# A new order in front of a fused conv and quantised-dense kernel: kernel blocks first, split convs, an early bias row

## The chip, the cores and the metric

One core of a Trainium2 chip. The metric is device microseconds of one execution. The engines are TensorE (PE; PEld is its weight load), VectorE (DVE), ScalarE (ACT), GpSimd (POOL) and the queue engine SyncE (SP). Each works through its own list of instructions in order; they meet only at semaphores.

## What is computed

`x` is 64 samples of 64 channels of 1024. A grouped convolution (9 taps, 4 groups) with a term from `cond` gives rows, these go through a dense layer whose operands are rounded to 8-bit levels, and the rounded result is added to `x`:

```
h  = conv1d(x, weight, groups=4, padding=4) + (cond @ c_weight.T)[:, :, None] + cbias
hq = fake_quant(h, 8 bits, per row)           # round(h / s) * s, s = absmax / 127
kq = fake_quant(kernel, 8 bits, per column)   # kernel is 1024 x 1024
y  = hq @ kq + fake_quant(bias, 16 bits, per row)
out = x + fake_quant(y, 8 bits, per row)
```

## The kernel before

The work is 32 tiles of 128 rows (8 samples x 16 channels of one group). The dense kernel comes as 8 blocks of 128 columns, loaded in four pairs of 1 MB. Step k of each engine's hand-written list handles several tiles at once: conv(k) on TensorE, the levels of tile k, dense of tile k - 2 for its first 512 columns (h = 0), dense of tile k - 4 (k - 3 and k - 2 later on) for its second half (h = 1), and the output of an older tile. `seconds(k)` gives the tiles whose second half falls in step k: one each, but two in steps 13 and 18, so that `outs(k)`, the y that are rounded in step k, has two in steps 15 and 20.

What a tile passes through:
- SP loads `xwin`; ScalarE rounds it to `x_hi` (`round_x`); POOL makes `x_lo = xwin - x_hi` (`split`, L229). SP's next load of a slot waits for that split.
- TensorE's `conv(t)` (L404): two select matmuls, then four matmuls each with x_hi and w_hi, x_hi and w_lo, x_lo and w_hi. The last four wait for `lo_made`.
- VectorE's `column_max(t)` (L602), TensorE's `spread_max(t)` (L429), VectorE's `levels(t)` (L619): the inverse, and the rounding of half of the tile to `a_int`; the other half is ScalarE's `round_levels(t)` (L325), four instructions.
- TensorE's `turn_levels(t)` (L437) transposes the integers into `turn_ps`, ScalarE's `take_levels(t)` (L317) copies them to `a_t`, and `dense(t, h)` (L447) multiplies with `kq` into bank h of `dense_ps`.
- VectorE's `scale_half(t, h)` and `add_bias` (VectorE for h = 0, POOL for h = 1), VectorE's `out_scale`, ScalarE's `quantise(t)` (two instructions, L335), POOL's `add_x(t)`, SP's store.

The kernel blocks come in front, among the first steps. VectorE's `k_levels(pair)` (L555) takes the absolute maximum of a pair, its scale and inverse, and rounds those of its blocks that are in `DVE_K`; ScalarE's `k_round(fb)` rounds the blocks in `ACT_K`. TensorE's `k_turn(user)` (L461) transposes a block into a bank of `dense_ps`, and ScalarE's `k_take(user)` copies it from there to `kq`. There are ten users, in the order of `K_USERS`: eight blocks, and two that spread the scales over the partitions ("scale0", "scale1"). A turn waits for an earlier user's take, so that its bank is free. `b_row`, the bias on all 128 partitions, is loaded late by SP, and `bias_scale` and `bias_levels` work on it in steps 1 and 2.

TensorE's list in front is, before: warm_up, ctx matmuls, warm_up, conv(0), k_turns 0-1, spread(0), conv(1), k_turns 2-4, spread(1), turn_levels(0), conv(2), dense(0,0), turn_levels(1), k_turns 5-6, spread(2), conv(3), k_turns 7-8, dense(1,0), turn_levels(2), spread(3), k_turn 9, conv(4), turn_levels(3), dense(2,0), spread(4), dense(0,1), conv(5). VectorE's: k_levels(0), column_max(0), k_levels(1), levels(0), column_max(1), k_levels(2), levels(1), bias_scale, column_max(2), k_levels(3), scale_half(0,0), levels(2), and so on.

Of the kernel before, what the change touches and what calls it, by code (L numbers as in the profile page):

```python
# [13 lines left out]
P = 128  # L14
# [7 lines left out]
NS = P // CG  # L22
# [10 lines left out]
ACT_K = (1, 3)  # L33
DVE_K = (0, 2, 4, 5, 6, 7)
# [4 lines left out]
def build(nc, xw, xr, wt, cond_t, cw_t, cond_bias, ker, bias, out):  # L39
    with ExitStack() as ctx:  # L40
# [6 lines left out]
        def sem(name):  # L47
# [27 lines left out]
        b_row = sb("b_row", [P, F], F32)  # L75
# [27 lines left out]
        turn_ps = ps("turn_ps", [P, NS, P], I16)  # L103

# [5 lines left out]
            "k_turned", "k_taken", "b_max_made", "b_scale_made", "b_inv_made",  # L110
# [53 lines left out]
        def _(sp):  # L164
# [51 lines left out]
        def _(pool):  # L216
# [50 lines left out]
        def _(act):  # L267
            act.dma_start(condt[:], cond_t).then_inc(s["cond_in"], 16)
# [40 lines left out]
            def bias_levels():  # L309
                act.wait_ge(s["b_inv_made"], 1)  # L310
                act.activation(b_int[:], b_row[:], ACT.Copy, scale=b_stat[:, 2:3]
# [45 lines left out]
            for k in range(second_step(LAST) + 2):  # L357
                if k == 2:
                    take_levels(1)
                    k_take(5)  # L360
                    k_take(6)
                    round_x(4)
                    bias_levels()
                elif k == 3:
                    k_take(7)
                    k_take(8)
                    take_levels(2)
                    round_x(5)
                else:
                    if k == 4:  # L370
                        k_take(9)
                    if there(k - 1):
                        take_levels(k - 1)
                    if there(k + 2):
                        round_x(k + 2)
                if k == 0:
                    k_round(3)
                    k_take(2)
                    k_take(3)
                    k_take(4)  # L380
                for t in outs(k):
                    quantise(t)
                if there(k):
                    round_levels(k)
            quantise_last()

        @block.tensor
        def _(pe):
            def warm_up():
                for i in range(WARM):  # L390
                    pe.matmul(dense_ps[:, 1, :].rearrange("p (i f) -> p i f", f=P), ident[:],
# [4 lines left out]
            warm_up()  # L396
            pe.wait_ge(s["cond_made"], 1)
# [6 lines left out]
            def conv(t):  # L404
                at, g, n0 = t % 2, t % GROUPS, t // GROUPS * NS
                x_at = t % XSPLIT
                wait(pe, "a_rounded_dve", t - 1)
                wait(pe, "a_rounded", t - 1)
                wait(pe, "hi_made", t + 1)
                for hs in range(2):  # L410
                    ns = slice(n0 + hs * NH, n0 + (hs + 1) * NH)
                    mm = pe.matmul(  # L412
                        conv_ps[:, at, hs, :].rearrange("p (n b) -> p n b", n=NH),
                        ctx2[:, g].rearrange("k q o -> k (q o)"),
                        select[:, ns].unsqueeze(2).to_broadcast([P, NH, BLOCKS]),
                        start=True, stop=False, skip_group_check=True)
                for x, w in ((x_hi, w_hi), (x_hi, w_lo), (x_lo, w_hi)):
                    if x is x_lo:
                        wait(pe, "lo_made", t + 1)
                    for ch in range(2):  # L420
# [6 lines left out]
                mm.then_inc(s["conv_made"], 1)  # L427
# [9 lines left out]
            def turn_levels(t):  # L437
                wait(pe, "a_rounded_dve", t + 1)
                wait(pe, "a_rounded", t + 1)
                wait(pe, "a_made", t)  # L440
                for j in range(NS):
# [5 lines left out]
            def dense(t, h):  # L447
# [5 lines left out]
                if t == 0:  # L453
                    pe.wait_ge(s["k_taken"], k_taken_of(f"scale{h}"))
# [6 lines left out]
            def k_turn(user):  # L461
                wait(pe, "k_taken", user if user > 5 else user - 1)
# [21 lines left out]
            pe.wait_ge(s["w_lo_made"], 2)  # L484
# [7 lines left out]
            for k in range(TILES):  # L492
                again = seconds(k)
                if k == 4:
                    k_turn(9)
                conv(k)
                if k == 0:
                    k_turns(0, 1)
                if k == 1:
                    k_turns(2, 4)  # L500
                if k == 3:
                    k_turns(7, 8)
                if k in (2, 3):
                    dense(k - LAG, 0)
                    turn_levels(k - 1)
                    if k == 2:
                        k_turns(5, 6)
                    spread_max(k)
# [240 lines left out]
```

## Time and profile before

| | |
|---|---|
| three runs, median (lowest to highest) | 283.77 us (283.61 to 284.38) |
| profiled execution, its own time | 282.26 us |
| its span, first to last instruction | 280.5 us |
| mean granted TensorE clock | 0.976 of full speed |
| busy: PE, DVE, ACT, POOL | 253.2, 211.9, 185.0, 194.2 us |
| HBM | 38.99 MB read, 16.78 MB written |

The rows below come from the page of this execution and from its trace. A granted clock of 1.00 is 2.4 GHz and 0.50 is 1.2 GHz. The busy time of an engine is the union of its instructions; TensorE's instructions overlap in the pipeline, so the time that one group costs is read from its start to the start of the next. A line in order of time may stand for several like instructions (x4): its second number is then the time from the first's start to the last's end. "[1.63 <-ACT x_hi L291]" is idle time ahead of it and what ended it.

### The profile page before, as it was taken

Reading aid. Unit: us, or ns where it says so; the run is one execution under the profiler, and the core shown is the slowest. Engines: PE = TensorE matmul, PEld = TensorE weight load, DVE = VectorE, ACT = ScalarE, POOL = GpSimd, SP = SyncE. Lnnn points to the kernel's source line nnn. Section 1 sums busy time; section 2 is a strip of 40 time slices with the busy share of each in tenths; the row PEclk is TensorE's granted clock in tenths of the full one; section 3 lists DMA queues with packets and bytes.
Section 4 is the critical chain, followed back from the end, with each engine's and each line's share of the span. In section 5 each row is a group of like instructions: output and inputs, shape, how many; then the busy total and the mean of one; then the engine's idle time right before and its main releaser. Section 6 shows DMA issues by size and latency. Waiting matters only on the chain.

```text
span 280.5 us, 4237 instructions
## 1 busy us (share of the span) xinstructions
PE 253.2 (90%) x1372; PEld 165.0 (59%) x1372; DVE 211.9 (76%) x447; ACT 185.0 (66%) x278; POOL 194.2 (69%) x104
## 2 busy tenths in 40 slices
PE   7966869999999999999899999799999999999800
PEld 3555557666666666666566566566666666665300
DVE  2598974668777778777978677967778888777674
ACT  4257686446777767667986567867777777755662
POOL 3533332544888888879897788997888888845973
PEclk9979999999999999999999999999999999999975
DMA  6999323530566665646677645565666664444424
GB/s 230 407 411 355 103 92 141 167 137 0 196 220 199 222 211 201 195 167 198 226 272 256 188 155 198 211 239 213 227 225 225 221 232 152 150 151 152 151 116 183
DMA packets 15800, 56.05 MB, mean 200 GB/s; under 512 B 1954, under 2 KB 1954, under 8 KB 15778
## 3 DMA queue, kind: packets, MB, share of 16 engines
q1 hardware_dynamic: 15488, 55.71, 56.2%
q8 instruction: 11, 0.18, 0.3%
q10 hardware_dynamic: 290, 0.07, 0.1%
q14 instruction: 11, 0.09, 0.1%
HBM read 38.99 MB, written 16.78 MB: 199 GB/s over the span
## 4 chain that ended last, share of the span: by engine, by line
POOL 49%; issue 41%; DVE 3%; DMA 3%; ACT 1%; SPq 0%; POOLq 0%; DVEq 0%; PE 0%
POOL x_lo L233 26%; POOL y L241 15%; POOL o_sb L249 8%; DMA k_raw<-ffn_kernel 3%; DVE k_max L558 1%; ACT kq L305 1%; DVE o_sb L665 1%; DVE y_max L656 0%; ACT x_hi L291 0%; SPq L175 0%; DVE k_int L569 0%; DVE dense_ps L590 0%; ACT y_int L349 0%; DVE y L599 0%; DVE last_max L673 0%
## 5 line engine op out<-in xcount | busy, mean ns | idle before, releaser
L456 PE MATMUL dense_ps<-kq,a_t 128*128 128x512 bf16 x496 | 116.7, 379 | 0.0
L233 POOL TENSOR_TENSOR x_lo<-xwin,x_hi 128x1032 fp32r<-128x1032 f32 x32 | 76.6, 2393 | 51.6 <-ACT x_hi L291 51.6
L249 POOL TENSOR_TENSOR o_sb<-y,o_sb 128x1024 f32<-128x1024 f32 x31 | 73.9, 2386 | 24.6 <-ACT y L341 24.6
L456 PEld LDWEIGHTS dense_ps<-kq,a_t 128*128 128x128 bf16 x496 | 47.6, 101 | 45.1 <-issue 0.3
L604 DVE TENSOR_REDUCE small_ps<-conv_ps 128x8 f32<-128x1024 f32 x32 | 39.4, 1232 | 39.6 <-PE conv_ps L422 39.5
L321 ACT CAST a_t<-turn_ps 128x1024 bf16<-128x1024 int16 x32 | 32.4, 1012 | 48.7 <-PE turn_ps L442 48.7
L338 ACT ACTIVATE y_int<-y,y_inv 128x1024 int16<-128x1024 f32 x31 | 35.6, 1147 | 24.1 <-DVE y_inv L647 24.1
L241 POOL TENSOR_TENSOR y<-y,bq 128x512 f32<-128x512 f32 x33 | 41.8, 1273 | 1.0 <-DVE y L590 1.0
L656 DVE TENSOR_REDUCE y_max<-y 128x1 f32<-128x1024 f32 x31 | 37.5, 1211 | 2.3 <-POOL y L241 2.0
L330 ACT ACTIVATE a_int<-conv_ps,inv 128x128 int16<-128x128 f32 x128 | 36.1, 363 | 1.9 <-DVE inv L625 1.9
L291 ACT CAST x_hi<-xwin 128x1032 fp32r<-128x1032 f32 x32 | 33.8, 1055 | 5.3 <-DMA xwin<-x_windows 5.3
L341 ACT ACTIVATE y<-y_int,y_scale 128x1024 f32<-128x1024 int16 x31 | 35.7, 1151 | 1.0
L422 PE MATMUL conv_ps<-x_hi,w_hi 128*128 128x512 f32 x128 | 36.3, 406 | 0.0
L422 PE MATMUL conv_ps<-x_hi,w_lo 128*128 128x512 f32 x128 | 35.8, 401 | 0.0
L422 PE MATMUL conv_ps<-x_lo,w_hi 128*128 128x512 f32 x128 | 35.2, 397 | 0.0
L422 PEld LDWEIGHTS conv_ps<-x_hi,w_lo 128*128 128x128 f32 x128 | 24.5, 192 | 6.2
L422 PEld LDWEIGHTS conv_ps<-x_hi,w_hi 128*128 128x128 f32 x128 | 25.0, 196 | 5.0
L422 PEld LDWEIGHTS conv_ps<-x_lo,w_hi 128*128 128x128 f32 x128 | 24.1, 188 | 6.1
L412 PE MATMUL conv_ps<-select,ctx 128*128 128x512 f32 x64 | 26.0, 489 | 1.6 <-ACT x_hi L291 1.6
L590 DVE SCALAR_TENSOR_TENSOR dense_ps<-dense_ps,row_scale,k_scale_b 128x512 f32<-128x512 f32 x31 | 23.1, 744 | 4.9 <-PE dense_ps L456 4.9
L442 PE MATMUL turn_ps<-ident_b,a_int 128*128 128x128 bf16 x256 | 19.8, 220 | 5.2 <-issue 3.5
L590 DVE SCALAR_TENSOR_TENSOR y<-dense_ps,row_scale,k_scale_b 128x512 f32<-128x512 f32 x31 | 23.0, 743 | 1.4 <-PE dense_ps L456 1.4
(62 smaller groups left out, 209.1 us busy)
## 6 DMA issues: line engine op xcount, KB each, us to landing
xwin<-x_windows SPq DMA_DIRECT2D x32, 516.0 KB, 4.7
o_sb<-x_rows SPq DMA_DIRECT2D x32, 512.0 KB, 4.5
out<-o_sb SPq DMA_DIRECT2D x31, 512.0 KB, 2.9
k_raw<-ffn_kernel SPq DMA_DIRECT2D x4, 1024.0 KB, 11.9
w_raw<-taps SPq DMA_DIRECT2D x2, 256.0 KB, 3.0
b_row<-ffn_bias SPq DMA_DIRECT2D x1, 512.0 KB, 15.1
out<-o_sb SPq DMA_DIRECT2D x2, 256.0 KB, 2.7
condt<-cond_t ACTq DMA_DIRECT2D x1, 32.0 KB
```

The lines of the kernel that those rows point to most:

```text
L233: pool.tensor_tensor(x_lo[:, at].rearrange("p n b -> p (n b)"), xwin[:, t % XWIN, :], x_hi[:, at].bitcast(F32).rearrange("p n b -> p (n b) ...
L241: pool.tensor_tensor(y[:, t % YRING, half(h)], y[:, t % YRING, half(h)], bq[:, half(h)], ALU.add).then_inc(s["biased1" if h else "biased0_ ...
L249: pool.tensor_tensor(o_sb[:, at, :], y[:, t % YRING, :], o_sb[:, at, :], ALU.add).then_inc(s["o_made"], 1)
L291: act.copy(x_hi[:, t % XSPLIT].rearrange("p n b -> p (n b)"), xwin[:, t % XWIN, :]).then_inc(s["hi_made"], 1)
L330: ins = act.activation(a_int[:, at, n * BLOCKS:(n + 1) * BLOCKS], conv_cols(at)[:, n, :], ACT.Copy, scale=inv8[:, at, n:n + 1])
L338: act.activation(y_int[:, t % 2], y[:, t % YRING, :], ACT.Copy, scale=y_inv[:, t % 2:t % 2 + 1]).then_inc(s["y_rounded"], 1)
L341: act.activation(y[:, t % YRING, :], y_int[:, t % 2], ACT.Copy, scale=y_scale[:, t % 2:t % 2 + 1]).then_inc(s["y_dequantised"], 1)
L422: mm = pe.matmul(conv_ps[:, at, hs, :].rearrange("p (n b) -> p n b", n=NH), w[:, ch, g].rearrange("p q o -> p (q o)"), x[:, x_at, hs * NH: ...
L456: mm = pe.matmul(dense_bank(t, h), a_t[:, t % LEVELS, q].rearrange("b j o -> b (j o)"), kq[:, q, half(h)], start=(q == 0), stop=(q == Q - 1))
L590: dve.scalar_tensor_tensor(out=to, in0=dense_bank(t, h), scalar=row_scale[:, t % RSRING:t % RSRING + 1], in1=k_scale_b[:, half(h)], op0=AL ...
L604: dve.tensor_reduce(cmax_ps, conv_ps[:, t % 2].rearrange("p h (n b) -> p (h n) b", b=BLOCKS), AX_X, ALU.max, apply_absolute_value=True).th ...
L656: dve.tensor_reduce(y_max[:, at], y[:, t % YRING, :], AX_X, ALU.max, apply_absolute_value=True).then_inc(s["y_max_made"], 1)
```

## The change

- The bias is loaded as one row (4 KB) by ScalarE's queue, first of all. After the first warm-up TensorE spreads it over the partitions with two fp32 matmuls of one row into both banks of `dense_ps`; VectorE and ScalarE read it there. `bias_scale` is VectorE's work ahead of the ctx instructions, `bias_levels` ScalarE's behind round_x(0). SP's loads are now x(2) ahead of k pair 3.
- `ACT_K` is (0, 1, 5, 7), `DVE_K` (2, 3, 4, 6). The scales of a pair are two instructions of one column.
- "scale0" is the third of `K_USERS` and has a bank of its own, `turn_ps`.
- conv is in two parts for tiles 1 to 4: `conv_start` (select and x_hi with w_hi), `conv_rest`.
- Tiles 0 and 1 are rounded by VectorE alone (`WHOLE = 2`).
- POOL's split(1), split(3) and split(4) wait for VectorE's 2nd, 3rd and 4th block rounding.
- The lists of the first five steps are written out anew on TensorE, VectorE and ScalarE.
- On ScalarE, in a step with two y, round_levels stands between the two quantises.

```diff
-ACT_K = (1, 3)
-DVE_K = (0, 2, 4, 5, 6, 7)
+ACT_K = (0, 1, 5, 7)
+DVE_K = (2, 3, 4, 6)
+WHOLE = 2
...
         def k_bank(user):
-            return dense_ps[:, user % 2 if user < 5 else 1, :]
-
-        K_USERS = (0, 1, 2, 3, "scale0", 4, 5, 6, 7, "scale1")
+            if user == 2:
+                return turn_f32
+            return dense_ps[:, 0 if user in (0, 3) else 1, :]
+
+        K_USERS = (0, 1, "scale0", 2, 3, 4, 5, 6, 7, "scale1")
...
             load_k(2)
+            load_xwin(2)
             load_k(3)
-            load_xwin(2)
-            sp.dma_start(b_row[:], bias.partition_broadcast(P)).then_inc(s["b_in"], 16)
             load_xwin(3)
...
             def split(t):
                 wait(pool, "hi_made", t + 1)
+                wait(pool, "k_rounded_dve", {1: 2, 3: 3, 4: 4}.get(t, 0))
                 wait(pool, "conv_made", t - XSPLIT + 1)
...
         def _(act):
+            act.dma_start(b_row[:], bias.unsqueeze(0)).then_inc(s["b_in"], 16)
             act.dma_start(condt[:], cond_t).then_inc(s["cond_in"], 16)
...
             round_x(0)
+            bias_levels()
+            k_round(0)
             k_round(1)
-            k_take(0)
-            k_take(1)
             round_x(1)
...
+            for user in range(5):
+                k_take(user)
+            round_x(2)
+            take_levels(0)
+            round_x(3)
+            take_levels(1)
+            round_x(4)
+            k_round(5)
+            k_take(5)
+            round_levels(2)
+            take_levels(2)
+            k_take(6)
+            round_x(5)
+            k_round(7)
+            round_levels(3)
+            k_take(7)
+            k_take(8)
+            take_levels(3)
+            k_take(9)
+            round_x(6)
+            round_levels(4)
+            for k in range(5, second_step(LAST) + 2):
+                if there(k - 1):
+                    take_levels(k - 1)
+                if there(k + 2):
+                    round_x(k + 2)
+                for t in outs(k)[:1]:
                     quantise(t)
                 if there(k):
                     round_levels(k)
+                for t in outs(k)[1:]:
+                    quantise(t)
...
             warm_up()
+            pe.wait_ge(s["b_in"], 16)
+            for h in range(2):
+                pe.matmul(dense_ps[:, h, :], ones[0:1, :], b_row[:, half(h)], start=True, stop=True
+                          ).then_inc(s["b_spread"], 1)
...
             def k_turn(user):
-                wait(pe, "k_taken", user if user > 5 else user - 1)
+                wait(pe, "k_taken", user if user >= 5 else (0, 0, 0, 1, 2)[user])
+                if user == 0:
+                    pe.wait_ge(s["b_rounded"], 1)
...
+            conv(0)
+            k_turns(0, 2)
+            conv_start(1)
+            k_turns(3, 4)
+            spread_max(0)
+            conv_rest(1)
+            turn_levels(0)
+            conv_start(2)
+            spread_max(1)
+            conv_rest(2)
+            turn_levels(1)
+            dense(0, 0)
+            conv_start(3)
+            spread_max(2)
+            conv_rest(3)
+            k_turn(5)
+            turn_levels(2)
+            dense(1, 0)
+            k_turn(6)
+            conv_start(4)
+            spread_max(3)
+            conv_rest(4)
+            k_turns(7, 8)
+            turn_levels(3)
+            k_turn(9)
+            dense(2, 0)
+            spread_max(4)
+            dense(0, 1)
+            for k in range(5, TILES):
...
-                dve.tensor_scalar(k_scale[:, fs], k_max[:, fs], 1.0 / 127, TINY, ALU.mult,
-                                  ALU.max).then_inc(s["k_scale_made"], 1)
-                dve.wait_ge(s["k_scale_made"], pair + 1)
+                for fb in (2 * pair, 2 * pair + 1):
+                    dve.tensor_scalar(k_scale[:, fb:fb + 1], k_max[:, fb:fb + 1], 1.0 / 127, TINY,
+                                      ALU.mult, ALU.max).then_inc(s["k_scale_made"], 1)
...
             k_levels(0)
-            for k in range(TILES):
+            k_levels(1)
+            column_max(0)
+            levels(0)
+            column_max(1)
+            levels(1)
+            column_max(2)
+            scale_half(0, 0)
+            k_levels(2)
+            levels(2)
+            add_bias(0, 0)
+            column_max(3)
+            scale_half(1, 0)
+            k_levels(3)
+            levels(3)
+            add_bias(1, 0)
+            for k in range(4, TILES):
```

## Rows read from the trace of the kernel before

**Rows 1.** Busy times by stretch: length, engines' busy us (x instructions), granted clock, DMA share, GB/s.
```profile
16.00:17.70 1.70, 0.09 (x1) 0.00 (x0) 1.70 (x1) 1.66 (x2) 0.00 (x0) 1.00 1.02 406
...
17.70:21.10 3.40, 3.38 (x8) 2.72 (x9) 3.30 (x5) 0.25 (x1) 2.38 (x1) 0.50 1.03 414
...
39.45:42.70 3.25, 1.04 (x17) 0.86 (x17) 2.06 (x3) 2.79 (x6) 1.11 (x1) 1.00 0.32 98
...
60.00:67.34 7.34, 7.34 (x42) 4.82 (x41) 5.19 (x12) 3.17 (x7) 3.66 (x3) 1.00 0.00 0
...
130.00:150.00 20.00, 18.59 (x104) 12.14 (x103) 15.59 (x34) 15.00 (x25) 17.91 (x9) 1.00 0.61 216
```

**Rows 2.** In order of time, the front: start, us, engine, line, operation; then idle time and releaser.
```profile
6.19 3.78 PE L391 MATMUL dense_ps<-ident 128*128 128x512 f32 x4
...
6.30 0.22 DVE L542 CAST ctx_r<-small_ps 128x64 fp32r<-128x64 f32 x1 [4.07 <-PE small_ps L400]
...
7.08 0.69 DVE L547 TENSOR_TENSOR ctx<-small_ps,ctx_r 64x512 fp32r<-64x512 f32 x1
...
29.41 1.21 DVE L575 TENSOR_REDUCE b_stat<-b_row 128x1 f32<-128x1024 f32 x1
...
30.84 0.17 DVE L581 RECIPROCAL b_stat<-b_stat 128x1 f32<-128x1 f32 x1
```

**Rows 3.** In order of time: VectorE's kernel levels, a split beside one, and a scale_half.
```profile
17.74 2.38 POOL L233 TENSOR_TENSOR x_lo<-xwin,x_hi 128x1032 fp32r<-128x1032 f32 x1 [6.18 <-ACT x_hi L291]
...
17.82 2.32 DVE L561 TENSOR_SCALAR k_scale<-k_max 128x2 f32<-128x2 f32 x1
...
24.25 2.27 DVE L558 TENSOR_REDUCE k_max<-k_raw 128x2 f32<-128x2048 f32 x1
...
26.96 1.42 DVE L569 TENSOR_SCALAR k_int<-k_raw,k_inv 128x1024 int16<-128x1024 f32 x2
...
36.73 0.75 DVE L590 SCALAR_TENSOR_TENSOR dense_ps<-dense_ps,row_scale,k_scale_b 128x512 f32<-128x512 f32 x1
```

**Rows 4.** In order of time: ScalarE's first two takes.
```profile
14.79 1.93 ACT L305 CAST kq<-dense_ps 128x1024 bf16<-128x1024 int16 x2 [0.32 <-PE dense_ps L478]
```

**Rows 5.** In order of time: TensorE in a steady step, and the second scale turn.
```profile
45.14 1.11 PE L469 MATMUL dense_ps<-ident,k_scale 128*128 128x128 f32 x8
...
60.59 0.78 PE L412 MATMUL conv_ps<-select,ctx 128*128 128x512 f32 x2
...
62.16 1.11 PE L422 MATMUL conv_ps<-x_hi,w_lo 128*128 128x512 f32 x4
...
64.05 0.62 PE L442 MATMUL turn_ps<-ident_b,a_int 128*128 128x128 bf16 x8
...
64.51 1.89 PE L456 MATMUL dense_ps<-kq,a_t 128*128 128x512 bf16 x8
...
66.23 0.33 PE L433 MATMUL small_ps<-col_max,same_b 128*128 128x64 f32 x2
```

**Rows 6.** In order of time: dense(0,0), and the beginning of conv(5).
```profile
31.08 1.90 PE L456 MATMUL dense_ps<-kq,a_t 128*128 128x512 bf16 x8
...
53.26 0.78 PE L412 MATMUL conv_ps<-select,ctx 128*128 128x512 f32 x2
```

**Rows 7.** In order of time: step 15, the second quantise's neighbours and TensorE's turn.
```profile
137.41 0.21 DVE L625 RECIPROCAL inv<-small_ps 128x8 f32<-128x8 f32 x1
...
139.56 1.12 ACT L330 ACTIVATE a_int<-conv_ps,inv 128x128 int16<-128x128 f32 x4
...
140.79 0.61 PE L442 MATMUL turn_ps<-ident_b,a_int 128*128 128x128 bf16 x8 [1.41 <-issue]
...
141.43 1.01 ACT L321 CAST a_t<-turn_ps 128x1024 bf16<-128x1024 int16 x1 [0.74 <-PE turn_ps L442]
```

**Rows 8.** In order of time: two groups of conv(1) at the lower clock.
```profile
18.73 1.91 PE L422 MATMUL conv_ps<-x_hi,w_hi 128*128 128x512 f32 x4
...
20.45 1.42 PE L422 MATMUL conv_ps<-x_hi,w_lo 128*128 128x512 f32 x4
```

More of the change, by code:

```diff
@@ L310, in bias_levels @@
                 act.wait_ge(s["b_inv_made"], 1)
[L311 removed]
+                act.activation(b_int[:], bias_ps, ACT.Copy, scale=b_stat[:, 2:3]
                                ).then_inc(s["b_rounded"], 1)
@@ L402, in _, with terms @@
             warm_up()
[L404 to L417, printed above, removed]
+            def terms(t, pairs):
+                at, g, x_at = t % 2, t % GROUPS, t % XSPLIT
+                for x, w in pairs:
                     if x is x_lo:
                         wait(pe, "lo_made", t + 1)
+                    if t == 0 and w is w_lo:
+                        pe.wait_ge(s["w_lo_made"], 2)
                     for ch in range(2):
@@ L426, in conv, with conv_start, conv_rest @@
                                 start=False, stop=False, skip_group_check=True)
-                mm.then_inc(s["conv_made"], 1)
+                return mm
+            def conv_start(t):
+                at, g, n0 = t % 2, t % GROUPS, t // GROUPS * NS
+                wait(pe, "a_rounded_dve", t - 1)
+                wait(pe, "a_rounded", t - 1 - WHOLE)
+                wait(pe, "hi_made", t + 1)
+                for hs in range(2):
+                    ns = slice(n0 + hs * NH, n0 + (hs + 1) * NH)
+                    pe.matmul(
+                        conv_ps[:, at, hs, :].rearrange("p (n b) -> p n b", n=NH),
+                        ctx2[:, g].rearrange("k q o -> k (q o)"),
+                        select[:, ns].unsqueeze(2).to_broadcast([P, NH, BLOCKS]),
+                        start=True, stop=False, skip_group_check=True)
+                terms(t, ((x_hi, w_hi),))
+            def conv_rest(t):
+                terms(t, ((x_hi, w_lo), (x_lo, w_hi))).then_inc(s["conv_made"], 1)
+            def conv(t):
+                conv_start(t)
+                conv_rest(t)
             def spread_max(t):
@@ L438, in turn_levels @@
                 wait(pe, "a_rounded_dve", t + 1)
-                wait(pe, "a_rounded", t + 1)
+                wait(pe, "a_rounded", t + 1 - WHOLE)
                 wait(pe, "a_made", t)
+                if t == 0:
+                    pe.wait_ge(s["k_taken"], k_taken_of("scale0"))
                 for j in range(NS):
@@ L453, in dense @@
                 if t == 0:
-                    pe.wait_ge(s["k_taken"], k_taken_of(f"scale{h}"))
+                    pe.wait_ge(s["k_taken"], len(K_USERS) * (h + 1) // 2)
                 for q in range(Q):
@@ L683, in _ @@
             k_levels(0)
-            for k in range(TILES):
+            k_levels(1)
[14 more added lines that the diff above has]
+            for k in range(4, TILES):
                 again = seconds(k)
                 column_max(k)
-                if k < 3:
-                    k_levels(1 + k)
                 if len(again) == 2:
@@ L692, in _ @@
                     out_scale(t)
-                if there(k - LAG):
-                    scale_half(k - LAG, 0)
+                scale_half(k - LAG, 0)
                 levels(k)
-                if k == 1:
-                    bias_scale()
-                if there(k - LAG) and not pool_adds(k - LAG, 0):
+                if not pool_adds(k - LAG, 0):
                     add_bias(k - LAG, 0)
-                if again:
-                    scale_half(again[-1], 1)
+                scale_half(again[-1], 1)
             out_scale(LAST - 3)
```

98 lines of the change are left out of this document (28 added, 70 removed).

## The prediction

> **What bounds the kernel now.** I read the page first (TensorE the busiest at 90%), then the busy times by stretch, then the engines in order of time for the front, one steady step and one step with two y. From about 53 us on TensorE has no gap: in a steady step it is busy for the whole 7.34 us, while VectorE, ScalarE and GpSimd leave room [rows 1]. So every microsecond by which a steady step begins later is a microsecond at the end. There are two exceptions. In the front TensorE waits for others, and conv(5), before which both orders do the same set of work, starts at 53.26 us [rows 6]. In the two steps with two y (k = 15 and 20) TensorE stands before turn_levels: there it is busy 18.59 of 20 us [rows 1]. The forecast therefore has two questions: when does conv(5) start, and what do these two steps save? The tail has the same instructions in both kernels and I leave it as it is.
>
> **The bias, early.** Removed is a 512 KB load behind the k loads. Added are two fp32 matmuls of 512 columns with a single row. Two such matmuls with 128 rows are the warm-up: four records over 3.8 us, the next instruction 3.4 us after the first [rows 2]. The rows fix no lower price for one row, so I take 3.4 us (bounds 1.7, if the clock is already at its upper level, and 3.8). They sit between the warm-up that ends at 5.0 us and the ctx matmuls, so ctx_mm comes at about 9.7 instead of 6.3 us. VectorE first does the bias scale, 1.6 us from its reduce to the end of its reciprocal, then the three ctx instructions, 1.5 us [rows 2]: 8.7 + 1.6 + 1.5 gives 11.9 us for the start of k_levels(0), which stood at 10.6. That is +1.3 us. The idle second warm-up and the wait for x_windows no longer hide it. ScalarE's two bias instructions run from 10.4 to 12.7 us, while it would wait for k_inv anyway; they cost nothing there, and 2.3 us if k_inv were earlier. With the 512 KB gone and x(2) ahead of k pair 3, x(2) and x(3) land earlier and that pair at most 1.3 us later, at about 21 us; VectorE wants it after 40 us, so the move costs nothing.
>
> **Kernel blocks first.** On VectorE k_levels of a pair costs 2.7 us from the reduce to the first rounding, 0.15 more because the scale is now two instructions, and 0.7 per rounding [rows 3]. With ACT_K at four blocks, pair 0 has no rounding on VectorE, and pairs 1, 2 and 3 have two, one and one. k_levels(0) ends at 14.8, k_levels(1) at 19.1, column_max(0) at 20.6 us. split(1) is held until 19.2 and ends at 21.6 (2.4 us [rows 3]). ScalarE's instructions over a whole tile or block cost 1.0 to 1.15 us: a take 0.97 [rows 4], four level roundings over half a tile 1.12 [rows 7]. It rounds blocks 0 and 1 from 14.8 to 17.1, x(1) until 18.2, then does five takes (the scale one, over half the columns, 0.6) with waits for the turns until 22.8, and x(2) until 23.9. So conv_start(2) (1.57 us [rows 5]) runs 23.9 to 25.5. spread(1) follows, and levels(1), 0.5 us up to the inverse and some 1.2 us for the whole tile's rounding (two halves of 0.69 us are the upper bound; a PSUM reduce over as many elements is 1.23 us), ends at 27.4. turn_levels(1) takes 0.46 and dense(0,0) 1.89 us to its last write [rows 5]. I call its end D0: 29.9 us. In the kernel before it is 31.08 + 1.90 = 33.0 us [rows 6]. Before, the clock fell to its lower level in the stretch from 17.7 to 21.1, after TensorE had been almost idle from 16 on [rows 1]. TensorE will again have gaps at that place; low there, D0 moves to about 31.5. I take 30.7 (29.4 to 31.5). Up to here the new order is ahead by 2.3 us.
>
> **Splits held back: the new serial chain.** This is where I expect the loss. split(3) now waits for the third VectorE rounding, which is block 4, in k_levels(2). k_levels(2) stands on VectorE's queue behind scale_half(0,0), which waits for D0. But conv_rest(3) needs split(3), and it stands on TensorE's queue ahead of everything later. From D0:
> - scale_half 0.7, k_levels(2) to the end of its rounding 2.7 + 0.15 + 0.75: D0 + 4.3 [rows 3]; scale_half lasts 0.75 there, and I let the next begin 0.7 after its start.
> - split(3) 2.4: D0 + 6.8. TensorE has only conv_start(3), spread(2) and the w_lo half to do, 1.57 + 0.17 + 0.95 = 2.7 us [rows 5]. It stands still for about 4.2 us.
> - The x_lo half 0.95, k_turn(5) seen by ScalarE some 0.65 us after its start (as the take of levels behind its turn [rows 7]), k_take(5) 0.97: D0 + 9.4. Only behind that take does ScalarE's queue have round_levels(2), 1.15 us [rows 7]; TensorE's turn_levels(2) waits for it, another 2.4 us of standing.
> - turn_levels 0.46, dense(1,0) 1.89: D1 = D0 + 13.05.
>
> Then it repeats, since k_levels(3) is behind scale_half(1,0) and split(4) waits for block 6: the x_lo half of conv(4) starts at D1 + 6.9, k_turn(7) at D1 + 7.8, and each of k_turn(8) and k_turn(9) waits for the take of the user before it (D1 + 9.5, D1 + 11.25). The second scale turn is some 0.9 us [rows 5], then dense(2,0) 1.72, spread 0.17, dense(0,1) 1.55: conv(5) at D1 + 15.55. With the clock up throughout, that is D0 + 28.6, against D0 + 20.3 before (53.26 - 33.0).
>
> **Why hold them.** In the trace a k_scale instruction of two elements took 2.32 us, ending with the POOL split that had started 0.08 us ahead of it; the same form beside an idle POOL belongs to the 2.7 us above [rows 3]. The new scale instructions have one element; the 0.15 us y_scale of that shape is my price for them. The hold also keeps a rounding clear of a split, and can save at most one split, 2.4 us, each time. Here the x for split(3) is ready about 26 us, long before that rounding, so the hold buys nothing and gives 7 us away. The Trainium skill (SBUF — State Buffer, section "SBUF: two separate sides") says that VectorE in a two-port mode and GpSimd exclude each other and the later one blocks fully. The two instructions that end together agree with it; by that rule too an unheld split(3) would be over before the rounding begins, and the sum without the hold would be some 4 us lower per split.
>
> **The clock.** A stand of 4.2 us is longer than the 1.6 us around 16 us after which the clock was low for 3.4 us; a stretch with 1.04 of 3.25 us busy kept it high [rows 1], so this isn't certain. At the lower level four conv matmuls take 1.72 us from start to start instead of 0.95 [rows 5, 8], 1.8 times. The TensorE work on the chain from D0 to D1 is 0.95 + 0.46 + 0.46 + 1.72 = 3.6 us, so low throughout adds 3.0. For the second part I add 1.0 (0 if high, 3.5 if most of it is low).
>
> **Steps with two y.** In step 15 inv is there at 137.6, but ScalarE does both quantises first and round_levels from 139.56; TensorE, done with conv at 139.2, starts turn_levels at 140.79 [rows 7]. With the levels between, round_levels would run from 137.65 to 138.8 and the gap of 1.55 us goes. The second quantise ends 1.4 us later, at 141.1; add_x of that tile, the add_bias and the split behind it on POOL shift as much, but that split is for a conv a full step away. take_levels and the next round_levels are up to 1.2 us late on ScalarE, which may cost 0.2. Gain 1.3 to 1.55 a step; two steps: 2.9.
>
> **Sum.** conv(5) at 30.7 + 13.05 + 3.0 + 15.55 + 1.0 = 63.3 us, against 53.3: +10.0. Less 2.9: +7.1. The profiled execution was 282.26 us (span 280.5), 1.5 below the median of 283.77; on the median the sum is 290.9.
>
> **Rivals.**
> - Chain as above, the clock stays up (or nearly): 29.9 + 28.6 = 58.5, +5.2 - 2.9 = +2.3, 286.1 us. For it: the stretch at 39.45 us kept its clock. Against it: the stand is longer.
> - Faster: the hold doesn't bind, the front is only TensorE's work. Then from D0 there are some 17 us of matmuls to conv(5) (two convs 6.9, two turns and four block turns 2.8, three denses 5.0, scale turn and spreads 1.2, waits for takes about 1): 30.7 + 17 = 47.7, -5.6 - 2.9, 275.3 us. It needs block 4 rounded by D0 + 0.3, that is k_levels(2) begun 3.3 us before D0. In the trace before, VectorE does that pair at 24.25 us [rows 3]; in the new queue it is behind the scale_half that waits for D0. I see no way round it, except an order that I misread.
> - The gain at two y doesn't come: POOL is busy 17.91 of 20 us there [rows 1], and a late add_x could hold the next step. Then +10.0: 293.8 us.
> - Within the noise: a short chain and a D0 of 29.4 or earlier leave a fraction of a microsecond.
>
> **Chances.** Chain with a low clock 0.55, chain with a high clock 0.27, no gain at two y 0.07, hold doesn't bind 0.08, within noise 0.03. This kernel's runs lie within about 0.3% (0.85 us), which I take as the bound of no change: faster 0.08, same 0.03, slower 0.89. The range: from D0 29.4, no low clock, 3.1 gained (285.4) to D0 31.5, all low, 2.6 gained (294.8); 285 to 295.
>
> **What the new profile would show.** Right: k_levels(2)'s reduce just behind scale_half(0,0); split(3) and split(4) starting as block 4's and block 6's roundings end; TensorE's waits at the x_lo half with POOL as releaser, about 4 us twice, and for k_taken; conv(5) at 58 to 66 us; no gap at steps 15 and 20; a low granted clock somewhere between 35 and 55 us. Wrong: conv(5) before 53 us, split(3) starting with its hi_made, or the gaps at the two y still there.

## The result, and the profile after

| | before | after |
|---|---|---|
| median, four runs each | 283.81 us | 289.15 us (288.31 to 289.43) |
| ratio to before, 95% interval | | 1.0202 (1.0143 to 1.026) |
| profiled execution (span) | 282.26 (280.5) us | 288.96 (287.2) us |
| conv(5) starts | 53.26 us [rows 6] | 63.03 us |
| from there to the end of the span | 227.2 us | 224.2 us |

The change made the kernel 2% slower (interval 1.4 to 2.6%). In the two profiled executions 9.8 us are lost before conv(5) and 3.1 us won behind it, 6.7 us in all; the medians differ by 5.3 us, since the profiled execution of the kernel before was 1.5 us faster than its median.

The front of the changed kernel in order of time (start, us, engine, line, operation, then idle time and what ended it):

```profile
5.14 2.28 PE L409 MATMUL dense_ps<-b_row,ones 1*128 1x512 f32 x4
...
11.25 2.29 DVE L605 TENSOR_REDUCE k_max<-k_raw 128x2 f32<-128x2048 f32 x1
...
27.85 1.89 PE L484 MATMUL dense_ps<-kq,a_t 128*128 128x512 bf16 x8
...
29.78 0.76 DVE L628 SCALAR_TENSOR_TENSOR dense_ps<-dense_ps,row_scale,k_scale_b 128x512 f32<-128x512 f32 x1 [0.73 <-PE dense_ps L484]
...
30.44 2.27 DVE L605 TENSOR_REDUCE k_max<-k_raw 128x2 f32<-128x2048 f32 x1
...
33.20 0.75 DVE L617 TENSOR_SCALAR k_int<-k_raw,k_inv 128x1024 int16<-128x1024 f32 x1
...
34.09 2.36 POOL L238 TENSOR_TENSOR x_lo<-xwin,x_hi 128x1032 fp32r<-128x1032 f32 x1 [7.96 <-DVE k_int L617]
...
36.50 2.08 PE L427 MATMUL conv_ps<-x_lo,w_hi 128*128 128x512 f32 x4 [4.24 <-POOL x_lo L238]
...
39.49 1.01 ACT L311 CAST kq<-dense_ps 128x1024 bf16<-128x1024 int16 x1 [5.14 <-PE dense_ps L508]
...
40.40 1.15 ACT L336 ACTIVATE a_int<-conv_ps,inv 128x128 int16<-128x128 f32 x4
...
41.65 0.61 PE L470 MATMUL turn_ps<-ident_b,a_int 128*128 128x128 bf16 x8 [2.19 <-issue]
...
42.09 1.89 PE L484 MATMUL dense_ps<-kq,a_t 128*128 128x512 bf16 x8
...
50.75 2.08 PE L427 MATMUL conv_ps<-x_lo,w_hi 128*128 128x512 f32 x4 [3.72 <-POOL x_lo L238]
...
54.81 1.03 PE L508 MATMUL dense_ps<-ident_b,k_int 128*128 128x128 bf16 x8 [1.10 <-ACT kq L311]
...
56.95 2.07 PE L499 MATMUL dense_ps<-ident,k_scale 128*128 128x128 f32 x8 [0.25 <-ACT kq L311]
...
58.81 2.68 PE L484 MATMUL dense_ps<-kq,a_t 128*128 128x512 bf16 x8
...
63.03 0.78 PE L441 MATMUL conv_ps<-select,ctx 128*128 128x512 f32 x2
```

dense(0,0) ends at 27.85 + 1.89 = 29.74 us (D0), 3.2 us ahead of the kernel before [rows 6]. From there the lines read as a chain: scale_half, the k reduce right behind it, block 4's rounding, and split(3) 0.14 us after that rounding ends, with "7.96 <-DVE k_int" as its idle time. TensorE has then stood 4.24 us for it. Next are the take of block 4, round_levels(2) directly behind that take, and turn_levels(2) after 2.19 us of standing. dense(1,0) ends at 43.98 us (D1). The second round, with split(4), ends in 3.72 us of standing and two waits for takes.

TensorE's waits of the changed kernel up to 64 us (us in total, times, longest):

```profile
PE conv_ps L427 <- POOL x_lo L238: 8.0, 2, 4.2
...
PE turn_ps L470 <- issue: 2.2, 1, 2.2
...
PE dense_ps L508 <- ACT kq L311: 1.1, 1, 1.1
```

Busy times by stretch of the changed kernel (length, then PE, PEld, DVE, ACT and POOL busy with their instruction counts, granted clock, DMA share, GB/s):

```profile
34.00:38.00 4.00, 1.50 (x4) 1.17 (x4) 1.63 (x6) 0.35 (x1) 2.36 (x1) 0.81 0.15 30
...
38.00:42.00 4.00, 1.81 (x17) 1.19 (x16) 1.46 (x2) 2.06 (x5) 0.00 (x0) 0.76 0.63 235
...
50.00:54.00 4.00, 2.96 (x12) 1.97 (x12) 1.14 (x1) 0.26 (x1) 3.04 (x2) 0.52 0.56 202
...
54.00:58.00 4.00, 2.94 (x21) 2.68 (x22) 0.32 (x2) 2.68 (x3) 0.00 (x0) 0.50 0.87 324
...
130.00:150.00 20.00, 20.00 (x111) 13.44 (x110) 16.69 (x38) 15.33 (x24) 15.91 (x9) 1.00 0.56 187
```

The clock is low in part of 34 to 42 us and for nearly all of 50 to 58 us. In the kernel before it was high from 30 to 60 us, also where TensorE was busy for only 2.55 of 4 us:

```profile
34.00:38.00 4.00, 2.55 (x18) 2.25 (x19) 3.86 (x11) 3.29 (x5) 0.00 (x0) 1.00 0.62 234
...
50.00:54.00 4.00, 4.00 (x21) 2.32 (x20) 3.23 (x9) 3.04 (x6) 1.93 (x1) 1.00 0.78 267
```

From 130 to 150 us TensorE is now busy for all 20 us, where it was 18.59 [rows 1]. The reason is in step 15, in order of time:

```profile
146.07 1.15 ACT L347 ACTIVATE y<-y_int,y_scale 128x1024 f32<-128x1024 int16 x1
...
147.44 1.14 ACT L336 ACTIVATE a_int<-conv_ps,inv 128x128 int16<-128x128 f32 x4 [0.22 <-DVE inv L663]
...
148.46 1.16 ACT L344 ACTIVATE y_int<-y,y_inv 128x1024 int16<-128x1024 f32 x1
...
149.00 0.62 PE L470 MATMUL turn_ps<-ident_b,a_int 128*128 128x128 bf16 x8
```

round_levels (L336) stands between the two quantises (L347 is the end of the first, L344 the start of the second), and TensorE's turn_levels starts at 149.00 us, as soon as conv(16) is through, without the 1.41 us of [rows 7].

### The profile page after: what moved, and what is told of

It reads as the page before. It is cut to its first block, busy times and chain, and to the rows that moved or that the text cites. A ratio compares the mean times of both kernels' runs of the same rounds, so it can differ in the third digit from the quotient of the medians.

```text
span 287.2 us, 4243 instructions
## 1 busy us (share of the span) xinstructions
PE 259.0 (90%) x1376; PEld 167.8 (58%) x1376; DVE 210.4 (73%) x449; ACT 185.3 (65%) x272; POOL 193.9 (67%) x104
## 4 chain that ended last, share of the span: by engine, by line
POOL 44%; issue 40%; DVE 2%; POOLq 0%; ACT 0%; DVEq 0%
POOL x_lo L238 21%; POOL y L246 14%; POOL o_sb L254 9%; DVE o_sb L704 1%; DVE y_max L695 0%; DVE dense_ps L628 0%; ACT y_int L355 0%; DVE y L637 0%; DVE last_max L712 0%; DVEq L41 0%; POOLq L132 0%; POOLq L253 0%; DVE y_scale L683 0%; DVE y_inv L686 0%; DVE y_max L718 0%
## 5 line engine op out<-in xcount | busy, mean ns | idle before, releaser
L344 ACT ACTIVATE y_int<-y,y_inv 128x1024 int16<-128x1024 f32 x31 | 35.6, 1150 | 23.7 <-DVE y_inv L686 23.7
L427 PE MATMUL conv_ps<-x_lo,w_hi 128*128 128x512 f32 x128 | 37.2, 414 | 8.0 <-POOL x_lo L238 8.0
L427 PE MATMUL conv_ps<-x_hi,w_lo 128*128 128x512 f32 x128 | 36.6, 408 | 0.0
L347 ACT ACTIVATE y<-y_int,y_scale 128x1024 f32<-128x1024 int16 x31 | 35.7, 1152 | 1.0
L336 ACT ACTIVATE a_int<-conv_ps,inv 128x128 int16<-128x128 f32 x120 | 33.8, 363 | 3.5 <-DVE inv L663 3.5
L427 PEld LDWEIGHTS conv_ps<-x_lo,w_hi 128*128 128x128 f32 x128 | 25.2, 198 | 15.0 <-POOL x_lo L238 8.9
L441 PE MATMUL conv_ps<-select,ctx 128*128 128x512 f32 x64 | 25.1, 475 | 0.7 <-DVE ctx L594 0.7
L672 DVE TENSOR_TENSOR a_int<-conv_ps,inv 128x512 int16<-128x512 f32 (+1 forms) x32 | 23.2, 725 | 0.0
```

The costliest lines, as they stand in the source:

```text
L336: ins = act.activation(a_int[:, at, n * BLOCKS:(n + 1) * BLOCKS], conv_cols(at)[:, n, :], ACT.Copy, scale=inv8[:, at, n:n + 1])
L344: act.activation(y_int[:, t % 2], y[:, t % YRING, :], ACT.Copy, scale=y_inv[:, t % 2:t % 2 + 1]).then_inc(s["y_rounded"], 1)
L347: act.activation(y[:, t % YRING, :], y_int[:, t % 2], ACT.Copy, scale=y_scale[:, t % 2:t % 2 + 1]).then_inc(s["y_dequantised"], 1)
L427: mm = pe.matmul(conv_ps[:, at, hs, :].rearrange("p (n b) -> p n b", n=NH), w[:, ch, g].rearrange("p q o -> p (q o)"), x[:, x_at, hs * NH: ...
```

## The experiments

Each was timed in rounds beside the kernel before on the same chip; the ratio is to those runs. "Rest" is the span less the start of conv(5).

| kernel | median us | ratio, 95% interval | conv(5) starts | span | rest |
|---|---|---|---|---|---|
| changed kernel | 289.15 | 1.0202 (1.0143 to 1.026) | 63.03 | 287.2 | 224.2 |
| no holds | 286.46 | 1.0135 (1.0082 to 1.0188) | 60.37 | 284.6 | 224.2 |
| hold of split(1) only | 283.23 | 1.0002 (0.996 to 1.0043) | 56.27 | 280.5 | 224.2 |
| k_levels early | 279.19 | 0.9899 (0.9832 to 0.9965) | 52.83 | 277.0 | 224.2 |
| k_levels early, hold of split(1) only | 278.75 | 0.9826 (0.9762 to 0.989) | 51.21 | 275.4 | 224.2 |
| TensorE kept busy in the stands | 285.49 | 1.011 (1.0041 to 1.0179) | 58.32 | 282.5 | 224.2 |
| bias late | 288.34 | 1.0167 (1.0119 to 1.0216) | 62.70 | 286.9 | 224.2 |
| two y in the old order | 293.35 | 1.0373 (1.0303 to 1.0443) | 64.43 | 291.7 | 227.3 |
| before, two y in the new order | 279.17 | 0.9825 (0.9765 to 0.9884) | 52.53 | 276.7 | 224.2 |
| before, one-column scales | 283.48 | 0.9999 (0.9962 to 1.0037) | 54.88 | 282.2 | 227.3 |
| best order found | 275.13 | 0.9685 (0.9637 to 0.9733) | 47.85 | 272.0 | 224.2 |

The rest is 224.2 us with the new order in the steps with two y and 227.2 or 227.3 without, whatever the front. So the two questions of the prediction can be read apart. Spans and starts are those of one profiled execution each; D0 and D1 below are the ends of dense(0,0) and dense(1,0) in it.

**No holds.**

```diff
-                wait(pool, "k_rounded_dve", {1: 2, 3: 3, 4: 4}.get(t, 0))
```

> The changed kernel without the holds: split(t) waits for x_hi alone. Theory 1 (the hold puts split(3) and split(4) behind scale_half and k_levels, and this chain sets conv(5)): split(3) and split(4) run as soon as their x_hi is there, the x_lo halves of conv(3) and conv(4) find them done, the two stands of about 4 us go, conv(5) at about 51 to 52 us instead of 63.0, time 277.5 to 279.5. A rounding of k_levels(1) may collide with split(1) and cost up to 1.7. Theory 2 (the low clock and the waits for the block takes are the cost, the hold only shows up in front of them): under 3 us are won, time above 286.

Measured: 286.46 us, conv(5) at 60.37. That is the number of Theory 2 (above 286, under 3 us won), though both stands at the x_lo halves are gone, as Theory 1 has it. Behind D0 the gain is there: 27.3 us from D0 to conv(5) instead of 33.3. Ahead of D0 3.3 us are lost. The trace of this kernel, in order of time, shows what took the place of the stands:

```profile
17.77 3.55 DVE L616 TENSOR_SCALAR k_int<-k_raw,k_inv 128x1024 int16<-128x1024 f32 x2
...
18.22 2.56 POOL L237 TENSOR_TENSOR x_lo<-xwin,x_hi 128x1032 fp32r<-128x1032 f32 x1 [4.50 <-ACT x_hi L296]
...
35.43 1.10 PE L426 MATMUL conv_ps<-x_lo,w_hi 128*128 128x512 f32 x4
...
37.44 0.61 PE L507 MATMUL dense_ps<-ident_b,k_int 128*128 128x128 bf16 x8 [0.90 <-DVE k_int L616]
...
46.78 2.40 POOL L237 TENSOR_TENSOR x_lo<-xwin,x_hi 128x1032 fp32r<-128x1032 f32 x1 [10.95 <-ACT x_hi L296]
...
47.26 0.21 DVE L608 TENSOR_SCALAR k_scale<-k_max 128x1 f32<-128x1 f32 x2
...
47.71 2.01 DVE L616 TENSOR_SCALAR k_int<-k_raw,k_inv 128x1024 int16<-128x1024 f32 x1
```

split(1) started at 18.22 us, while the first of the two roundings of k_levels(1) ran and ahead of the second. The pair took 3.55 us instead of 1.42, so that D0 came at 33.1 instead of 29.7 us. (In this execution k_levels(0) also began 1.0 us later, since the bias matmuls took 3.78 us instead of 2.28.) conv(3) ends without a wait, but block 4's turn, next in TensorE's list, still waits for its rounding, which still stands behind scale_half(0,0). A later split, at 46.78, made block 6's rounding take 2.01 us instead of 0.75. Theory 1 was right about the two stands, but its sum was 7 to 9 us too low: it had the first collision at 1.7 us where it was 2.1, nothing for the second (that split, of tile 5, was never held; it meets the rounding because the lists have shifted), nothing for the waits for takes that come next, and no low clock, which remained (granted clock 0.57 from 40 to 44 us, where dense(1,0) took 3.48 us).

**Only split(1) held.**

```diff
-                wait(pool, "k_rounded_dve", {1: 2, 3: 3, 4: 4}.get(t, 0))
+                wait(pool, "k_rounded_dve", {1: 2}.get(t, 0))
```

> The changed kernel with the hold of split(1) kept and those of split(3) and split(4) taken away. Without any hold the second rounding of k_levels(1) took about 2.9 us beside split(1). Theory: with split(1) held the two roundings take 1.42 us again, dense(0,0) ends at about 30 us instead of 33.1, conv(5) at about 58 us (it was 60.4 with no hold, 63.0 with all), 283.5 to 285. Rival (the collision is hidden by ScalarE's takes): within 0.5 us of the kernel without holds, 286.5.

Measured: 283.23 us, conv(5) at 56.27, D0 at 29.81: the two roundings of k_levels(1) take 1.42 us again. The last two holds cost 6.7 us of span (287.2 to 280.5), 5.9 on the medians. The hold of split(1) is worth keeping: conv(5) comes 4.1 us earlier than with no hold, of which 0.8 is the earlier start of k_levels(0) in this execution; the medians differ by 3.2. conv(5) and the time came out a little below the forecast (58 us, 283.5 to 285). TensorE's waits, over the whole run, show what then binds:

```profile
PE turn_ps L470 <- issue: 2.9, 2, 2.2
...
PE dense_ps L508 <- DVE k_int L617: 2.5, 2, 1.6
...
PE dense_ps L508 <- ACT kq L311: 1.8, 1, 1.8
```

It waits for block roundings, for takes, and for round_levels(2) behind the take of block 4. Those come from the place of k_levels and from the order of the lists, not from the hold, as the next run and the last one show.

**k_levels early, holds kept.**

```diff
             levels(1)
+            k_levels(2)
             column_max(2)
             scale_half(0, 0)
-            k_levels(2)
             levels(2)
             add_bias(0, 0)
+            k_levels(3)
             column_max(3)
             scale_half(1, 0)
-            k_levels(3)
             levels(3)
```

> The changed kernel with its holds, but on VectorE k_levels(2) stands before column_max(2) and k_levels(3) before column_max(3), so that neither waits for a dense. Theory 1 (it is the place of k_levels behind scale_half that makes the hold bite): split(3) starts at about 31 and split(4) at about 39 us, no stand over 1.5 us at an x_lo half, conv(5) at about 51.5 us, time about 277.5 (276.5 to 280). Theory 2 (the hold itself costs, wherever k_levels stands): under 3 us are won.

Measured: 279.19 us, 10 us faster than the changed kernel and 1% faster than the kernel before. In order of time:

```profile
28.80 2.27 DVE L605 TENSOR_REDUCE k_max<-k_raw 128x2 f32<-128x2048 f32 x1
...
35.03 1.10 PE L427 MATMUL conv_ps<-x_lo,w_hi 128*128 128x512 f32 x4
...
38.79 0.61 PE L470 MATMUL turn_ps<-ident_b,a_int 128*128 128x128 bf16 x8 [2.19 <-issue]
...
52.83 0.78 PE L441 MATMUL conv_ps<-select,ctx 128*128 128x512 f32 x2
```

The reduce of pair 2 starts at 28.80, before D0 (31.3 us here). The x_lo half of conv(3) follows its w_lo half without a wait. Theory 1 holds: with VectorE's roundings ahead of the denses the same holds cost nothing that TensorE waits for. The 2.19 us before turn_levels(2) stay. D0 is 1.5 us later than in the changed kernel's profile, and conv(5) still 10.2 us earlier.

**k_levels early, only split(1) held.** The two edits together.

> k_levels(2) and k_levels(3) early, as in the run with the early order, and only split(1) held. Theory (with k_levels early no x_lo half waited, so the two later holds neither cost nor give anything): 279.2, within 0.6, conv(5) at 52 to 53.5 us. Rival (split(3) or split(4) now meets the rounding of block 4 or 6 and blocks it, as split(1) did): up to 2 us slower, 281.

Measured: 278.75 us, within 0.6 us of the kernel with all holds, as the theory has it. The rival's collision did happen, but the other way round. In order of time:

```profile
28.28 0.75 DVE L617 TENSOR_SCALAR k_int<-k_raw,k_inv 128x1024 int16<-128x1024 f32 x1
...
28.36 2.91 POOL L238 TENSOR_TENSOR x_lo<-xwin,x_hi 128x1032 fp32r<-128x1032 f32 x1 [1.64 <-ACT x_hi L297]
```

Block 4's rounding had started 0.08 us ahead of split(4) and took its usual 0.75 us; the split took 2.91 us instead of 2.4. Nothing waited for it. The two profiled executions differ by more than the edit: here D0 came at 28.0 us instead of 31.3 (the spread matmuls took 2.17 us instead of 3.78, and conv(1) was already 3.3 us earlier), and behind D0 1.6 us were lost again, with dense(1,0) at 3.29 us instead of 1.89 and a granted clock of 0.78 from 34 to 38 us, where it was 1.00 with all holds.

**TensorE kept busy in the stands.** The result of the added matmuls is overwritten; otherwise this is the changed kernel.

```diff
 WARM = 2
+BUSY = 4
...
                 for x, w in pairs:
+                    if x is x_lo and t in (3, 4):
+                        wait(pe, "a_made", t - 1)
+                        for i in range(BUSY):
+                            pe.matmul(turn_f32.rearrange("p (i f) -> p i f", f=P), ident[:],
+                                      ident[:].unsqueeze(1).to_broadcast([P, JH, P]),
+                                      start=True, stop=True)
                     if x is x_lo:
                         wait(pe, "lo_made", t + 1)
```

> The changed kernel, with four fp32 warm-up matmuls (3.4 us of TensorE's time) written to the turn bank ahead of the x_lo half of conv(3) and of conv(4), where TensorE stands for about 4 us. The stands keep their length. If the low clock after the stands costs what its rows say (D0 to D1 14.2 us against 13.05 summed at the high clock, D1 to conv(5) 19.05 against 15.55), the granted clock stays at 1.00 from 30 to 60 us and up to 4.7 us are won: 284.5 to 286. If the clock costs little because TensorE is not what the chain waits for, within 1 us of 289.2.

Measured: 285.49 us (284.25 to 287.70), 3.7 us less than the changed kernel's median. The profiled execution, the fastest of the four, has 4.7 us less span and conv(5) at 58.32, with more work done. Busy times by stretch, the same stretches as above:

```profile
34.00:38.00 4.00, 3.20 (x16) 1.50 (x14) 1.88 (x7) 0.27 (x1) 2.36 (x1) 1.00 0.16 29
...
38.00:42.00 4.00, 1.76 (x15) 1.06 (x15) 1.12 (x2) 3.07 (x6) 0.00 (x0) 1.00 0.62 236
...
50.00:54.00 4.00, 2.24 (x28) 1.61 (x27) 1.46 (x2) 2.19 (x3) 1.68 (x1) 1.00 0.93 335
...
54.00:58.00 4.00, 3.95 (x23) 2.50 (x25) 1.15 (x6) 2.31 (x4) 1.30 (x1) 1.00 0.52 195
```

The clock is 1.00 in every stretch from 30 to 62 us. D0 to D1 takes 12.97 us and D1 to conv(5) 15.70, against 14.24 and 19.05 in the changed kernel. These are the prediction's sums at the high clock (13.05 and 15.55) to 0.15 us. So the low clock cost 1.3 us in the first part and 3.35 in the second of the changed kernel's profiled execution. By the medians it is 3.7 us, not 4.65: executions differ in how long the clock is low. All four runs are below all four of the changed kernel, but the two ratio intervals still overlap; the waits and the clock in the views carry this reading.

**Two y in the old order.** ScalarE's loop from step 5 on in the changed kernel, with both quantises ahead of round_levels.

> The changed kernel with ScalarE's order in the steps with two y as before (both quantises, then round_levels). Theory: TensorE stands 1.4 to 1.55 us before turn_levels in steps 15 and 20 again, +3.1 us, 292.2 (291.5 to 292.6). Rival (the gap came from the late front and would be hidden now): no change, 289.2.

Measured: 293.35 us; rest 227.3 instead of 224.2. The median is 1.1 us above the forecast; in the profiled execution conv(5) came 1.4 us later than in the changed kernel's. D0 is only 0.2 us later; 1.3 us are lost between D0 and D1, where the granted clock was 0.54, 0.50 and 0.68 in the stretches from 34 to 46 us instead of 0.81, 0.76 and 1.00. This edit touches nothing there, so it is the executions that differ.

**Before, with two y in the new order.** The same four lines, alone, in the kernel before.

> The kernel before, with nothing changed but ScalarE's order in the steps with two y (one quantise, round_levels, the other quantise). Theory: the two stands of TensorE at turn_levels go, -3.07 us, about 280.5 against 283.6 in the same runs, span from conv(5) to the end 224.2 instead of 227.2. Rival (the late second quantise holds POOL's add_x and the next step): less than 1.5 us.

Measured: 279.17 us, ratio 0.9825; rest 224.2 instead of 227.2, so 3.07 us from this edit. conv(5) was 0.7 us earlier in the profiled execution. This part of the change alone would have been a gain of some 1.1% by the rest.

**Bias late.** In the changed kernel: the 512 KB broadcast load behind k pair 3, no spread matmuls, `bias_scale()` behind column_max(2), `bias_levels()` behind round_x(4).

> The changed kernel with the bias as before: a 512 KB broadcast load behind k pair 3, no spread matmuls, bias_scale on VectorE behind column_max(2), bias_levels on ScalarE behind round_x(4), where ScalarE waits anyway. Theory (the early bias holds k_levels(0) up by 0.65 to 1.6 us and saves 1.6 us of VectorE's list ahead of scale_half(0,0), 0.7 of which it would idle there): k_levels(0) starts at 10.6 us, and conv(5) moves by -0.7 to +0.3 us, so 288.4 to 289.5 beside 289.15 for the changed kernel. Rival (the early bias is what makes the front slow): 2 us or more faster.

Measured: 288.34 us over six runs. k_levels(0) started at 9.79 us, 1.5 earlier; dense(0,0) ended at 28.83, 0.9 earlier; but scale_half(0,0) had to wait for bias_scale until 29.54, 0.24 earlier than in the changed kernel. conv(5) came 0.33 us earlier. Between D0 and D1 the clock was low for longer than in the changed kernel's profile (0.66, 0.50 and 0.56 in the stretches from 34 to 46 us), so a few tenths in the start of conv(5) can't be put down to the edit. The rival, 2 us or more, is out: the medians differ by 0.8 us. The place of the bias is worth less than a microsecond here.

**Before, with one-column scales.**

```diff
-                dve.tensor_scalar(k_scale[:, fs], k_max[:, fs], 1.0 / 127, TINY, ALU.mult,
-                                  ALU.max).then_inc(s["k_scale_made"], 1)
-                dve.wait_ge(s["k_scale_made"], pair + 1)
+                for fb in (2 * pair, 2 * pair + 1):
+                    dve.tensor_scalar(k_scale[:, fb:fb + 1], k_max[:, fb:fb + 1], 1.0 / 127, TINY,
+                                      ALU.mult, ALU.max).then_inc(s["k_scale_made"], 1)
+                dve.wait_ge(s["k_scale_made"], 2 * pair + 2)
```

> The kernel before with the scales of a pair as two one-column instructions, nothing else. Theory A (VectorE's two-column scale stood still for 2.1 to 2.3 us because it is in a form that a POOL split shuts out; the one-column form is not, but the rounding right behind it is): the scales take 0.2 us beside the split, and the rounding of block 2 ends some 0.5 us behind the end of the split, so that under 0.6 us are won. Theory B (only the scale was shut out): the rounding ends 2.1 us earlier, conv(5) up to 2 us earlier, about 281.7.

Measured: 283.48 us, ratio 0.9999: no change. In order of time:

```profile
17.70 2.39 POOL L233 TENSOR_TENSOR x_lo<-xwin,x_hi 128x1032 fp32r<-128x1032 f32 x1 [6.21 <-ACT x_hi L291]
...
17.79 0.21 DVE L562 TENSOR_SCALAR k_scale<-k_max 128x1 f32<-128x1 f32 x2
...
18.23 2.41 DVE L570 TENSOR_SCALAR k_int<-k_raw,k_inv 128x1024 int16<-128x1024 f32 x1
```

Theory A: the two scales take 0.21 us beside the split, where the two-column form took 2.32 [rows 3]; the rounding behind them takes 2.41 instead of 0.75 and ends 0.55 us after the split. The stall has only moved to the next instruction of a form that is shut out.

**Best order found.** From the kernel with k_levels early and split(1) held:

```diff
 ScalarE:
-            k_take(5)
             round_levels(2)
             take_levels(2)
+            k_take(5)
...
             k_take(7)
-            k_take(8)
             take_levels(3)
+            k_take(8)
             k_take(9)
 TensorE:
             conv_rest(3)
-            k_turn(5)
             turn_levels(2)
+            k_turn(5)
             dense(1, 0)
...
-            k_turns(7, 8)
+            k_turn(7)
             turn_levels(3)
-            k_turn(9)
+            k_turn(8)
             dense(2, 0)
+            k_turn(9)
```

> k_levels(2) and (3) early, only split(1) held, and in front turn_levels(2) and round_levels(2) ahead of block 4's turn and take, turn_levels(3) between the turns of blocks 6 and 7, dense(2,0) ahead of the last scale turn. Theory: the stand of 2.2 us before turn_levels(2) and those of 1.1 and 0.7 us before the turns, which wait for takes, are filled: conv(5) at 49 to 50.5 us instead of 52.8, 276 (275.5 to 277.5). Rival (VectorE's list is the bound of the front by now): within 1 us of 279.2.

Measured: 275.13 us, 0.4 below the forecast's range, ratio 0.9685: faster than both kernels. conv(5) starts at 47.85 us, 1.2 us earlier than expected. TensorE's waits over the whole run:

```profile
PE small_ps L459 <- DVE col_max L651: 1.4, 2, 1.1
...
PE turn_ps L470 <- issue: 0.7, 1, 0.7
...
PE dense_ps L508 <- ACT kq L311: 0.7, 1, 0.7
...
PE dense_ps L484 <- ACT k_scale_b L309: 0.6, 1, 0.6
```

None but the ident wait of 1.4 us at the start is longer than 1.1 us. Here too the rounding of block 4 started just ahead of split(4) (28.98 and 29.06 us) and the split took 2.91 us.

## Why the prediction was right

It forecast 290.9 us (285 to 295) and a loss; 289.15 us was measured. The mechanism, a chain over the holds with a low clock behind the stands, is what the runs show. The nearness of the number is in part luck, as errors of 1 to 2.5 us cancel. Step by step:

- **The bias, early.** 11.9 us forecast for k_levels(0) (its terms add up to 11.8), 11.25 in the profiled execution. The two spread matmuls took 2.2 us, inside the bounds (1.7 to 3.8); in the run without holds they took 3.7, and k_levels(0) started at 12.24. Their four records started 0.83, 0.43 and 0.43 us apart here, and 1.02, 0.85 and 0.86 us apart there. I read that as the clock's two levels, but the view gives 1.00 for both stretches, so the clock itself isn't shown there. A cost that I had missed is in the sum too: ctx's cast on VectorE (9.22 us) took 1.27 us instead of 0.49 before, and ended 0.27 us after POOL's w_lo, which ran from 7.73 to 10.22 us.
- **Kernel blocks first.** D0 summed to 29.9 us, 29.74 measured. I had then added 0.8 for a low clock in this part, which wasn't needed: the clock was low during conv(0) instead (0.50 from 12 to 16 us). That D0 came out so close is in part luck: the lead of 0.65 us with which k_levels(0) started went again in ScalarE's takes, which waited 0.40 and 0.81 us for turns. No run takes apart what the other changes of the front (ACT_K, the turns' order, the split convs, `WHOLE`) each gave to the 3.2 us by which D0 is earlier.
- **The serial chain.** The rounding of block 4 ends at D0 + 4.2 (4.3 forecast), TensorE stands 4.24 us (4.2) and 2.19 us before turn_levels(2) (2.4). The runs on holds and places show that it is the hold together with the place of k_levels: take the last two holds away and 6.7 us of span return, move k_levels and 10.2 return; with k_levels moved, taking them away changes the median by 0.4 us.
- **The clock.** 3.0 + 1.0 forecast (3.6 us at 1.8 times gives 2.9); the run with a busy TensorE gives 1.3 + 3.35 = 4.65. The sum was right by 0.65 us, the split wasn't: I took the first round to be low throughout, but dense(1,0) already ran at the high clock (42.09, 1.89 us), and the second round was low from 50 us on.
- **Steps with two y.** 2.9 forecast, 3.07 measured, by a run that adds this edit to the old kernel and one that takes it from the new. The late second quantise held nobody up; add_x waited 1.19 us for it and POOL caught up.
- **The sum.** conv(5) at 63.3 forecast, 63.03 measured. Its parts were off by more: D0 at 30.7 for 29.74, D0 to D1 16.05 for 14.24, D1 to conv(5) 16.55 for 19.05. These cancel, and that is luck. On spans the change cost 6.7 us (7.1 forecast), on medians 5.3. The terms of the range's upper end add up to 294.5, not 294.8, which changes nothing.
- **The rule of the Trainium skill** (SBUF — State Buffer, section "SBUF: two separate sides"): the traces agree. Each time a rounding began beside a running split, it ended 0.5 us after it (no holds: 20.78 and 21.32, 49.18 and 49.72; one hold: 45.59 and 46.13; before with one-column scales: 20.09 and 20.64). Where the rounding began first, it was the split that took longer (2.91 us, k_levels early with one hold). I used it to say that an unheld split(3) meets no rounding, which was right (those met were of k_levels(1), by split(1), and of block 6, by split(5)). But the sentence "some 4 us lower per split" was too much: with both later holds gone it is 6.7 us of span for the two (5.9 on the medians), since the next waits in TensorE's list took over. How much of it is clock isn't shown.
- **The faster rival** (275.3 us if the hold didn't bind) priced a front that is only TensorE's work. The lists as written never reach it even without the hold (286.46, or 283.23 with split(1) held); the best order found, with k_levels and several turns and takes moved, comes to 275.13.

## What to carry to other kernels

Before delaying an instruction to keep it clear of another, ask which queue its release stands in and what that queue waits for: here a 2.4 us collision was avoided by a wait that depended, over VectorE and TensorE, on the dense just ahead, and the engine that bounds the kernel stood 8 us. An early hold with its release close by (split(1)) paid; the two later ones didn't. Where one engine bounds everything behind a point, compare two orders by the time of that point and by the rest behind it: here each edit moved only one of them, but for differences between executions. And a stand on TensorE can cost more than its length: two stands of 4.24 and 3.72 us were followed by low clocks that cost another 4.65 us by the spans, 3.7 by the medians. How much differs: in the two runs with k_levels early the same stand of 2.19 us comes ahead of a dense(1,0) of 1.89 us in one and 3.29 in the other.

## What the runs showed of the hardware that I hadn't expected

- The four records of the one-row spread matmuls took 2.28 us in the changed kernel and 3.78 us in the run without holds, with the same instructions ahead of them. From 14 to 16 us the granted clock was 0.50 in the one and 1.00 in the other: where the clock is in front differs from one execution to the next.
- Filling two stands with 7.2 us of useless matmuls made the profiled execution 4.7 us shorter, the median 3.7.
- A two-column scale instruction beside a POOL split took 2.32 us and two one-column ones 0.21 us, though they do the same work.
- Whichever of a VectorE rounding and a POOL split began first kept its time, and the other took longer: 2.41 us for 0.75, or 2.91 for 2.4.
- The kernel before, over 37 runs on the three chips of these comparisons, lay between 280.49 and 285.29 us; differences under 0.5% rest on the spans and waits above, not on the medians.
